# Conv and transformer step on one Trainium2 core: the local product in another PSUM bank, the last norm chunk inside the feed-forward

## The reference

```python
x = x + _L0_conv_ref(_ln_c(x), wq, wk, wv, rel_x, rel_y)      # softmax over 49 neighbours
t = _to_tokens(x)
def step(h, p):
    op = jnp.argmax(h[0, 0, :NOPS])
    attn = softmax((h @ p['wq'][op]) @ (h @ p['wk'][op]).T * scale)
    h = jnp.where(p['am'][op], attn @ (h @ p['wv'][op]) @ p['wo'][op], h)
    z = relu(h @ p['w1'][op] + p['b1'][op]) @ p['w2'][op] + p['b2'][op]
    h = jnp.where(p['fm'][op], z, h)
t = t + scan(step, _ln_t(t))
```

## Time and profile before

| | us |
|---|---|
| median of 3 runs (lowest to highest) | 239.64 (239.6 to 239.88) |
| the profiled execution | 239.32 |
| its span, first to last instruction | 237.2 |
| PE busy | 222.1 (94%) |
| DVE busy | 158.4 (67%) |
| ACT busy | 156.1 (66%) |
| POOL busy | 26.2 (11%) |

### The profile page before, as it was taken

One profiled execution on the slowest core, in us unless ns is written; L12 is line 12 of the kernel. 1 busy time (PEld: TensorE's weight loads), 2 busy tenths in 40 slices (PEclk: granted clock), 3 DMA queues, 4 the chain that ended last, 5 costly groups with the idle time before them and its releaser, 6 DMA issues.

```text
span 237.2 us, 5409 instructions
## 1 busy us (share of the span) xinstructions
PE 222.1 (94%) x1995; PEld 153.4 (65%) x1996; DVE 158.4 (67%) x294; ACT 156.1 (66%) x304; POOL 26.2 (11%) x37
## 2 busy tenths in 40 slices
PE   7999799999899979999999999999999999998991
PEld 3376477666667665422666778887888888885230
DVE  1387456667757754664869999877779778743642
ACT  2573824767687785554589978699777777773641
POOL 9600321212121006200000000000000000000000
PEclk9999999999999999999999999999999999999999
DMA  5600000000000000001000000000000000000016
GB/s 148 146 3 0 3 6 0 3 0 3 19 15 3 1 3 0 0 4 39 7 3 0 1 3 0 3 1 3 0 3 0 3 0 1 3 3 0 0 34 145
DMA packets 3151, 3.60 MB, mean 15 GB/s; under 512 B 1077, under 2 KB 2229, under 8 KB 3126
## 3 DMA queue, kind: packets, MB, share of 16 engines
q1 hardware_dynamic: 2486, 2.59, 4.6%
q10 hardware_dynamic: 544, 0.66, 1.1%
q0 software_dynamic: 96, 0.00, 0.0%
HBM read 2.21 MB, written 1.05 MB: 14 GB/s over the span
## 4 chain that ended last, share of the span: by engine, by line
PE 77%; ACT 10%; DVE 7%; issue 5%; DVEq 0%; ACTq 0%
PE ps L680 12%; PE ps L666 12%; PE ps L645 12%; PE ps L733 6%; PE ps L747 6%; PE ps L507 4%; PE ps L495 4%; PE ps L469 3%; PE ps L381 2%; DVE negmax L1152 2%; ACT prob L862 2%; PE ps L346 2%; PE ps L425 2%; PE ps L369 2%; PE ps L626 2%
## 5 line engine op out<-in xcount | busy, mean ns | idle before, releaser
L999 ACT COPY arena<-ps 128x1024 f32<-128x1024 f32 x32 | 32.3, 1010 | 16.1 <-PE ps L666 15.9
L645 PE MATMUL ps<-h_st,g_st 128*128 128x512 f32 x128 | 38.7, 424 | 0.7 <-ACT late L947 0.4
L1249 DVE TENSOR_REDUCE negmax<-ps 128x1 f32<-128x1024 f32 x32 | 38.4, 1218 | 1.4 <-PE ps L645 1.3
L947 ACT ACTIVATE late<-ps,negmax 128x1024 f32<-128x1024 f32 x32 | 35.8, 1119 | 4.9 <-DVE negmax L1249 4.4
L666 PE MATMUL ps<-eye,late 128*128 128x128 f32 x256 | 33.5, 274 | 0.6 <-DVE late L1259 0.2
L666 PEld LDWEIGHTS ps<-eye,late 128*128 128x128 f32 x256 | 29.1, 140 | 6.9 <-DVE late L1259 2.7
L680 PE MATMUL ps<-arena,late 128*64 128x128 f32 x512 | 31.5, 276 | 1.1 <-ACT arena L999 1.1
L680 PEld LDWEIGHTS ps<-arena,late 128*64 128x64 f32 x512 | 27.6, 137 | 3.8 <-issue 2.2
L862 ACT ACTIVATE prob<-ps,negmax 128x308 f32<-128x308 f32 x32 | 16.3, 514 | 20.9 <-DVE negmax L1152 20.9
L645 PEld LDWEIGHTS ps<-h_st,g_st 128*128 128x128 f32 x128 | 21.8, 188 | 8.9 <-issue 3.2
L1259 DVE TENSOR_SCALAR late<-late,rinv 128x1024 f32<-128x1024 f32 x32 | 24.1, 754 | 1.1
(11 more groups left out here) (125 smaller groups left out, 314.8 us busy)
## 6 DMA issues: line engine op xcount, KB each, us to landing
out<-osum SPq DMA_DIRECT2D x8, 128.0 KB, 2.4
x<-in_x SPq DMA_DIRECT2D x2, 256.0 KB, 5.2
x<-in_x ACTq DMA_DIRECT2D x2, 256.0 KB, 5.8
onehot<-in_key_onehot SPq DMA_DIRECT2D x2, 133.0 KB, 2.8
w1d<-in_ffn_w SPq DMA_DIRECT2D x4, 64.0 KB, 2.2
w2p<-in_ffn_pack SPq DMA_DIRECT2D x2, 65.5 KB, 1.9
spread_w<-in_spread_mat SPq DMA_DIRECT2D x4, 32.0 KB, 5.5
mean_w<-in_mean_mat SPq DMA_DIRECT2D x1, 96.0 KB, 2.3
```

Of the source, the lines that this page charges most:

```text
L645: mm = nc.tensor.matmul(ps[:, 2 * h + c, :], g_st[:, b2, h, q0:q0 + P], h_st[:, b2, h, part, c * 512:c * 512 + 512], start=(part == 0), st ...
L947: nc.scalar.activation(pr[:, n % 2, :], ps[:, 2 * (n % 2):2 * (n % 2) + 2, :], ACT.Exp, bias=negmax[:, 0, n % 2:n % 2 + 1], accum_out=rows ...
L999: nc.scalar.copy(prt[:, n // 8 % 2, n % 2, :, q0:q0 + P], ps[:, bank:bank + 2, :].rearrange("p b (c q) -> p (b c) q", c=4)).then_inc(S["s_ ...
L1249: nc.vector.tensor_reduce(negmax[:, 0, n % 2:n % 2 + 1], ps[:, 2 * (n % 2):2 * (n % 2) + 2, :], mybir.AxisListType.XY, ALU.max, negate=Tru ...
```

## The change

`mix` writes bank 6, columns 384 to 511, beside the turned values, and `add_mixed` reads it there. `mix(p)` waits until the values of pair p+1 are copied out of bank 6, and `turn_values(p+1)` until `add_mixed(p-1)` is done. The guards of bank 7 stand ahead of the next job that writes bank 7, one pair later. ACT copies the values of pair 1 ahead of the second half of the projected values.

When the first step is a feed-forward alone, `variance(1,3)`, `root` and the table load happen inside it: the variance between `up(0,0)` and `up(0,1)`, the root ahead of ACT's first relu, the table load behind its second, DVE's inverse behind its first relu. The dummy products and the finishing of the norm are left to the other branch. `turn_row(6)` comes ahead of `down(1)`, and DVE's `decide` one t earlier.

```diff
@@ -53,6 +53,7 @@
 W2COLS = 2 * C + 2 + 1
 TWICE = ((0, 0), (1, 0), (0, 1), (1, 1))
 RING = 15
+MIX0 = NCH * P
 CENTRE_AT = ((0, 1, 2, 3), (7, 7, 7, 7))
 VAR_AT = (((4, 0), (6, 0), (4, 0), (6, 0)), ((7, 0), (7, 0), (7, 0), (5, 0)))
 SPREAD_AT = ((((4, 5), 0), ((6, 7), 0), ((4, 5), 0), ((6, 7), 0)),
@@ -178,9 +179,9 @@
 
 
             name = eng.engine.name
-            op, entry, step, cur, last, stride, am, fm, alone, other, n_att, n_ffn, event = (
+            op, entry, step, cur, last, stride, am, fm, alone, n_att, n_ffn, event = (
                 eng.alloc_register(f"{name}_{k}")
-                for k in "op entry step cur last stride am fm alone other n_att n_ffn event".split())
+                for k in "op entry step cur last stride am fm alone n_att n_ffn event".split())
             for reg in (n_att, n_ffn, event, cur):
                 eng.reg_mov(reg, 0)
 
@@ -226,15 +227,14 @@
                 eng.reg_alu(alone, am, 1, op=ALU.logical_shift_left)
                 eng.reg_alu(alone, fm, alone, op=ALU.bitwise_and)
                 eng.reg_alu(alone, fm, alone, op=ALU.subtract)
-                if finish_norm:
-                    eng.reg_alu(other, alone, 2, op=ALU.bitwise_xor)
-                    with eng.If(eng.snap(other, min_val=0, max_val=2) > 0):
-                        finish_norm()
                 with eng.If(eng.snap(alone, min_val=0, max_val=2) > 0):
                     do_section(first or feed_forward, n_ffn)
                     eng.reg_add(event, event, 1)
                     if not loads_itself:
                         load_next()
+                if finish_norm:
+                    with eng.Else():
+                        finish_norm()
                 eng.reg_mov(last, step)
 
 
@@ -480,6 +480,8 @@
                 pe.wait_ge(S["v_staged"], p + 1)
                 if p > 0:
                     pe.wait_ge(S["vk_copied"], p)
+                if p > 1:
+                    pe.wait_ge(S["mixed"], p - 1)
                 for c in range(NCH):
                     mm = nc.tensor.transpose(ps[0:CH, 6, c * P:c * P + P],
                                              v_st[:, pp, c * CH:c * CH + CH], eye[:])
@@ -499,12 +501,12 @@
             def mix(p):
                 pp = p % 2
                 pe.wait_ge(S["pt_copied"], p + 1)
-                pe.wait_ge(S["vk_copied"], p + 1)
+                pe.wait_ge(S["vk_copied"], min(p + 2, NPAIR))
                 if p > 0:
                     pe.wait_ge(S["mixed"], p)
                 for c in range(NCH):
                     for h in range(2):
-                        mm = nc.tensor.matmul(ps[C * h:C * h + C, 7, 0:P],
+                        mm = nc.tensor.matmul(ps[C * h:C * h + C, 6, MIX0:MIX0 + P],
                                               v_key[0:CH, pp, c, C * h:C * h + C],
                                               prob_t[0:CH, pp, h, c, :],
                                               start=(c == 0), stop=(c == NCH - 1))
@@ -528,45 +530,52 @@
             scores(2)
             values(1)
             turn_values(1)
-            pe.wait_ge(S["v_copied"], 2)
             mix(0)
             for p in range(1, NPAIR - 2):
                 turn_probs(p)
                 turn_values(p + 1)
 
-                pe.wait_ge(S["mixed"], p)
+                if p == 1:
+                    pe.wait_ge(S["v_copied"], 2)
+                    biases(1, 0)
+                if p == 2:
+                    pe.wait_ge(S["bias_added"], 6)
+                    biases(1, 1)
+                if p == 3:
+                    pe.wait_ge(S["bias_added"], 8)
+                    queries(2)
+                if p == 4:
+                    pe.wait_ge(S["q_copied"], 3)
+                    values(2)
+                if p == 5:
+                    pe.wait_ge(S["v_copied"], 3)
+                    values(3)
+                if p == 6:
+                    pe.wait_ge(S["v_copied"], 4)
+                    queries(3)
                 if p == 7:
+                    pe.wait_ge(S["q_copied"], 4)
+                    pe.wait_ge(S["mixed"], 1)
                     turn_row(7, x2f)
-                if p in (8, 10, 12):
+                if p == 8:
+                    pe.wait_ge(S["decided"], 1)
+                    pe.wait_ge(S["mixed"], p)
+                    centre(0, 7)
+                if p in (10, 12):
+                    pe.wait_ge(S["var_copied"], p // 2 - 4)
+                    pe.wait_ge(S["mixed"], p)
                     centre(p // 2 - 4, 7)
                 if p in (9, 11, 13):
+                    pe.wait_ge(S["centre_copied"], (p + 1) // 2)
                     variance(1, (p - 9) // 2)
-                if p < 3:
-                    biases(1, p - 1)
-                if p in (3, 6):
-                    queries(2 + p // 6)
-                if p in (4, 5):
-                    values(p - 2)
                 if p == 6:
                     pe.wait_ge(S["q_copied"], 3)
+                    pe.wait_ge(S["bias_added"], 8)
                 if p == 10:
                     pe.wait_ge(S["q_copied"], 4)
                 scores(p + 2)
-
-                if p < 3:
-                    pe.wait_ge(S["bias_added"], 2 * p + 4)
-                if p in (3, 6):
-                    pe.wait_ge(S["q_copied"], 3 + p // 6)
-                if p in (4, 5):
-                    pe.wait_ge(S["v_copied"], p - 1)
-                if p == 7:
-                    pe.wait_ge(S["decided"], 1)
                 if p == 10:
                     load_next()
-                if p in (8, 10, 12):
-                    pe.wait_ge(S["centre_copied"], p // 2 + 1)
-                if p in (9, 11, 13):
-                    pe.wait_ge(S["var_copied"], (p - 7) // 2)
                 mix(p)
 
             turn_probs(14)
@@ -579,13 +588,14 @@
             spread(1, 2)
 
             pe.wait_ge(S["mixed"], NPAIR)
+            pe.wait_ge(S["var_copied"], 3)
             centre(3, 7)
-            keep_busy(6, 1)
             pe.wait_ge(S["h_ready"], 3)
-            variance(1, 3)
-            keep_busy(6, 2)
 
             def finish_norm():
+                keep_busy(6, 1)
+                variance(1, 3)
+                keep_busy(6, 2)
                 spread(1, 3)
 
 
@@ -750,6 +760,8 @@
                     mm.then_inc(S["hid_down"], 1)
 
                 up(0, 0)
+                if first:
+                    variance(1, 3)
                 up(0, 1)
                 if first:
                     up(1, 0)
@@ -764,8 +776,9 @@
                 up(2, 1)
                 pe.wait_ge(S["h_ready"], chunks + 5)
                 up(2, 0)
+                pe.wait_ge(S["relu_dve"], 8 * f + 3)
+                turn_row(6)
                 down(1)
-                turn_row(6)
                 up(3, 1)
                 pe.wait_ge(S["h_ready"], chunks + 6)
                 pe.wait_ge(S["decided"], a + f + 2)
@@ -893,8 +906,8 @@
             copy_turned(0)
             copy_values(0)
             exps(2)
+            copy_values(1)
             copy_projected(1)
-            copy_values(1)
             for p in range(1, NPAIR - 2):
                 copy_turned(p)
                 copy_values(p + 1)
@@ -917,8 +930,10 @@
             copy_turned(15)
             square(1, 3)
             copy_centred(1, 3)
-            root(1, 3)
-            load_table(ACT.Exp)
+
+            def finish_norm():
+                root(1, 3)
+                load_table(ACT.Exp)
 
             def attention(a, f, ev, row):
                 base = act.snap(NT * a)
@@ -1021,19 +1036,23 @@
                                          ACT.Identity, bias=w2p[:, 2 * C + 2:2 * C + 3]
                                          ).then_inc(S["h_ready"], 1)
 
+                if first:
+                    root(1, 3)
                 for t in range(4):
                     relu(t, 0)
                     if first and t == 1:
                         act.wait_ge(S["h_ready"], 4)
                         store(0)
                     relu(t, 1)
+                    if first and t == 0:
+                        load_table(ACT.Exp)
                     if t > 1 or (t == 1 and not first):
                         store(t - 1)
                 if first:
                     load_next(1)
                 store(3)
 
-            run(attention, feed_forward, None, partial(feed_forward, first=True), True)
+            run(attention, feed_forward, finish_norm, partial(feed_forward, first=True), True)
 
 
         @block.vector
@@ -1167,7 +1186,7 @@
                 dve.wait_ge(S["pv_done"], p + 1)
                 win = x2[:, b2:b2 + 1, BR * hb:BR * hb + BR, BC * xb:BC * xb + BC]
                 nc.vector.tensor_tensor(win, win,
-                                        ps[:, 7, 0:P].rearrange("p (a r c) -> p a r c", a=1, c=BC),
+                                        ps[:, 6, MIX0:MIX0 + P].rearrange("p (a r c) -> p a r c", a=1, c=BC),
                                         ALU.add).then_inc(S["mixed"], 1)
 
             def decide(n, bank, ev=None):
```

(6 more changed lines are left out.)

## The result

The changed kernel takes 236.18 us (median of 4 runs, 235.76 to 236.78) against 239.62: a ratio of 0.9866, 95% interval 0.9847 to 0.9886, so 3.4 us less. The profiled execution took 235.76, its span is 233.6 instead of 237.2.

What follows compares the result with a forecast made beforehand. PE itself was taken as the bound, stalling in the local product only before `mix`. Gains 2.0 + 2.0 - 0.43 + 0.1 = 3.7 us take 239.32 to 235.6; 0.32 for the median gives 235.9 us, range 234.6 to 238.0.

Steps and rivals of the forecast that it cites:

- Local product: Pair by pair, with `mix` in bank 6: 2.2 us of stalls given back, 0.2 taken off, 2.0 us gained.
- The listing's 0.8 for the three centred copies: Pairs 8, 10 and 12: stalls behind ACT's centred copies, 0.8 us in all, given back whole.
- the two deductions: Local product: 0.1 us off for ACT's values copies in pairs 9, 11, 13; 0.1 for `load_next` of pair 10.
- Pair 14: `mix(14)` newly waits for the values of pair 15: 0.4 us, covered by PE's 0.60 us idle for the root.
- Hand-over: Third scale to `up(0,0)`, dummies and a wait removed: start at 91.4 instead of 93.40, 2.0 us gained.
- rival 3: At the branch PE fetches code or spends most of SP's 1.86 us instead of 0.35: 237.4 us; chance 0.11.
- Inline variance: Inside the first feed-forward: four variance products of two passes come back on PE, 0.43 us lost, what follows covered.
- The choice: `decide` one t earlier, turned row ahead of `down(1)`: up to 0.15 us gained, 0.1 taken.
- rival 1: `turn_values` behind `add_mixed`, pairs 1 to 13: PE waits on bank 6, kernel slower, 240.7 us at 0.6 excess; chance 0.06.
- Rival 2: Local product: waits reappear at the next use of bank 7 or 6 and eat the 2.0: 237.9 us; chance 0.13.
- rival 4: Pairs 1, 2, 7 give stalls back whole, nothing lost to ACT, branch free: 235.0 us or a little under; chance 0.12.

Runs made afterwards that it cites:

- local_only: Only the local product's part of the change (bank 6, new waits, swapped copies) on the kernel before; hand-over and first feed-forward as before: 237.06 us.
- mix14_bank7: The changed kernel with the product of pair 14 alone back in bank 7, without its wait for the copy of pair 15's values: 236.43 us.
- no_dummies: The kernel before the change without its three dummy products around the variance, all else as it was: 240.06 us.
- late_wait: The changed kernel with PE's wait for the third scale moved from ahead of the branch to behind it: 235.44 us.
- row_back: The changed kernel with the turned row behind `down(1)` and the choice at t = 2, as before the change: 236.5 us.
- late_add: The changed kernel with one extra 128x512 DVE operation between the maximum and the add in pairs 3 to 6: 236.94 us.
- section_only: Only the change's second half (variance, root, table load inside the first feed-forward, earlier turned row); product in bank 7 as before: 238.62 us.
- variance_twice: The changed kernel with the four variance products in the section done twice, the first result overwritten: 237.49 us.
- late_wait_decided: late_wait with PE's wait for the choice moved ahead of the first of the two last `up`: 235.11 us.

## Why the prediction was right

The forecast was 235.9 and the time is 236.18; the sum had 3.7 us, the three stretches show 3.36. Its terms came out like this:

- **Local product: 2.0 predicted, 2.47 measured**, and `local_only` gives 2.45 by itself. By pairs, from the starts of `mix` against before, less the 0.33 of the start: pair 0 gains 0.03 (0.1 predicted); pairs 1 and 2 bring it to 1.04 by pair 3 (0.43 each predicted); pair 7 adds 0.56, read at the turned values behind it (0.44); pairs 8, 10 and 12 add 0.17, 0.37 and 0.37. The mechanism held: the stall of `mix` came back partly at `turn_values`, behind an add that is queued behind the maximum. The size was off in three places. Pairs 1, 2 and 7 gave back about 0.1 more each: the load follows the maximum's end by 0.31 instead of the 0.36 of the sum (35.19 to 35.50 in pair 1), and its product follows the load by 0.03 instead of 0.10. The listing's 0.8 for the three centred copies was too low (the products' modelled ends cover part of a stall; from start to start they are 0.91). And the two deductions, ACT's lag in pairs 9 to 13 and `load_next`, came to nothing: `mix(11)` gains 2.14 like `mix(10)`.
- **Pair 14** lost its 0.4 and had it covered, as worked out; mix14_bank7 shows it.
- **Hand-over: 2.0 predicted, 1.56 measured.** This is the step that was mis-sized: "the branch is nearest to this difference, so I take 0.35". From the third scale to the first `up` it took 0.93 where 0.49 stood in the sum. Rows of SP and DVE were taken for PE's price, because dummies ran over PE's own way through the branch; no_dummies shows that they covered it with no room. By the prediction's own sign, over 1 us between the third scale and `up(0,0)`, this came near to rival 3.
- **Inline variance: 0.43 predicted, 0.56 measured** (3.23 - 2.67). From start to start the variance takes 0.36 (1.06 to 1.42 behind the first `up`), and the repeat cost only 0.22. The other 0.20 is the broken stream of `up`: its step into the variance and its first step behind it take 0.53 each, where a step inside the stream takes 0.43.
- **The choice: 0.1 gain predicted, 0.11 lost.** The wait for the choice did go, but the turned row had been 0.2 us of cover for the store of chunk 1, on which the same `up` waits. With the row gone from there, the store and the passing of the second wait end last. That wait was named nowhere in the prediction.

The errors are +0.47, -0.44, -0.13 and -0.21, and they nearly cancel. The mechanisms held, except in the choice; that the total came so close is in part luck, since the two largest errors are opposite and of the same size.

The rivals: the ring (rival 1) exists, with 0.11 us of room left in an undisturbed pair after its hand-over of 0.12; it costs where DVE is late. Rival 2 falls with local_only. Rival 3 was half right in size: PE spends 0.9, not 1.86, and late_wait shows that it is passing time. Of rival 4 one part came: nothing was lost to ACT. On the fetch of code: the Trainium skill, Runtime: NRT & Kernel Launch, Instruction fetch mechanics, says that a taken branch to a target outside the window makes the engine wait for the target's code; in late_wait no idle time is left at the branch, so here PE did not stop, and no run shows whether the target lay outside. The same section calls the crossing of a block's boundary mostly hidden; if the 0.41 us of row_back is such a crossing, it was not hidden there.

What stays open: what DVE waits for in those 0.41 us, the 0.15 of C in late_add and section_only, the 0.3% of no_dummies, and the larger time outside the span in variance_twice.

## What to carry to other kernels

When a buffer's guard is moved, look for the next wait in the same engine's order before counting the stall as gain, and take the stall from start to start of the products. A wait that stands ahead of a branch puts the branch's own passing time behind it; put the wait behind the branch where the data allow it, and the satisfied one of two waits first. Work that seems to fill a gap (dummies, a small transpose) may be covering a sequencer or a store: ask what ends last when it goes.

## What was not expected of the hardware

- PE's way through the registers and one branch into the section took about 0.9 us from the last wait passed (88.08 to 89.00); with two branches and the variance to issue it took 1.4 (the variance's start at 92.30 to 93.71 in no_dummies).
- Of two waits in a row ahead of the last `up`, a second one that is long met cost PE time when it stood behind the one that ended last: 0.21 us from the event to the weights in the changed kernel (0.36 in section_only). With the late one behind it was 0.05 (104.21 to 104.26 in the kernel before), and with the met one moved away 0.05 as well (late_wait_decided).
- Forty instructions that do nothing at the start of DVE's program moved a stop of 0.41 us out of the path, 100 us later.
